# A macaron block on one NeuronCore: silu 1 ahead of the first HH, and attention's batch 0 prepared one round sooner in FFN 1

## The reference, cut to what matters

```python
# x: (8, 1024, 128)
x = x + 0.5 * ffn(layernorm(x))
x = x + attn(layernorm(x))
x = x + 0.5 * ffn(layernorm(x))

def ffn(x):                       # weights: int32 / 127, hidden size 384
    h = silu(x @ wg.T) * (x @ wu.T)
    return h @ wd.T

def attn(x):                      # 4 query heads, 2 key heads of 32
    h = rmsnorm(x) * norm_w
    q, k = l2norm(h @ Wq), l2norm(h @ Wk)
    p = softmax(causal(q @ k.T * exp(log_temperature)))
    return x + gate * ((p @ (h @ Wv)) @ Wo)
```

## Time and profile before

| | us |
|---|---|
| median of 3 runs (459.06 to 459.52) | 459.48 |
| the profiled execution | 459.42 |
| its span, first to last instruction | 457.6 |
| TensorE busy | 413.5 |
| ScalarE busy | 382.8 |
| VectorE busy | 354.2 |
| GpSimd busy | 260.6 |

### The profile page before, as it was taken

How to read it: one execution, slowest core, us unless ns; L and a number is a source line. 1 busy time by engine, 2 the same in 40 slices (tenths; PEclk the granted TensorE clock), 3 DMA queues, 4 the chain that set the end, 5 groups by cost and what they waited for, 6 DMA issues and landing times.

```text
span 457.6 us, 10470 instructions
## 1 busy us (share of the span) xinstructions
PE 413.5 (90%) x3747; PEld 214.1 (47%) x3747; DVE 354.2 (77%) x872; ACT 382.8 (84%) x546; POOL 260.6 (57%) x321
## 2 busy tenths in 40 slices
PE   0779998989998999999999999999999998999995
PEld 0346665663334335335335335345344244767554
DVE  5899997799499789689689689687647937878654
ACT  3799999667968988988988988988977998999961
POOL 5499999973444444444453553541131456998951
PEclk9999999999999999999999999999999999999999
DMA  5586433334026072084072072092070112557462
GB/s 161 127 163 149 65 53 69 70 71 96 20 53 134 1 140 48 1 140 47 0 138 46 0 138 47 1 139 48 1 139 0 24 26 49 136 93 139 93 116 74
DMA packets 119151, 34.94 MB, mean 76 GB/s; under 512 B 101569, under 2 KB 119105, under 8 KB 119105
## 3 DMA queue, kind: packets, MB, share of 16 engines
q1 hardware_dynamic: 117824, 34.02, 38.9%
q10 hardware_dynamic: 1280, 0.33, 0.3%
HBM read 4.98 MB, written 4.19 MB: 20 GB/s over the span
## 4 chain that ended last, share of the span: by engine, by line
PE 51%; issue 14%; ACT 12%; DVE 11%; POOL 7%; DMA 2%; DVEq 0%; SPq 0%; POOLq 0%; ACTq 0%
PE ps L507 11%; PE ps L706 11%; PE ps L687 9%; PE ps L711 9%; ACT XN L458 4%; PE ps L558 3%; PE ps L569 3%; ACT PT L817 3%; PE ps L594 2%; DVE H L327 2%; ACT SG L476 2%; DVE X L1021 2%; PE ps L691 2%; POOL OL L281 2%; DVE AN L1008 1%
## 5 line engine op out<-in xcount | busy, mean ns | idle before, releaser
L817 ACT ACTIVATE PT<-ps,k_exp 128x1024 f32<-128x1024 f32 (+1 forms) x192 | 162.0, 899 | 20.2 <-PE ps L691 14.8
L507 PE MATMUL ps<-XT,WT 128*128 128x512 f16 x384 | 95.0, 386 | 8.6 <-DVE H L327 3.1
L687 PE MATMUL ps<-QKT 128*128 128x512 f16 (+3 forms) x384 | 87.1, 328 | 11.4 <-ACT PT L817 9.3
L706 PE MATMUL ps<-PT,V 128*32 128x512 f32 (+3 forms) x768 | 81.8, 498 | 0.0
L711 PE MATMUL ps<-PT,ones 128*32 128x512 f32 (+3 forms) x768 | 79.6, 486 | 0.0
L433 POOL TENSOR_TENSOR HL<-H,HH 128x1024 f16<-128x1024 f32 x31 | 67.0, 2160 | 7.3 <-ACT HH L482 5.1
L327 DVE SCALAR_TENSOR_TENSOR H<-SG,k_isilu,ps 128x1536 f32<-128x1536 f32 x32 | 58.0, 1811 | 14.9 <-ACT SG L476 5.6
L281 POOL TENSOR_TENSOR OL<-ON,OH 128x512 f16<-128x512 f32 x15 | 18.2, 1216 | 77.4 <-ACT OH L277 77.4
L687 PEld LDWEIGHTS ps<-QKT 128*128 128x128 f16 x384 | 27.8, 97 | 69.2 <-ACT PT L817 60.1
L507 PEld LDWEIGHTS ps<-XT,WT 128*128 128x128 f16 x384 | 34.6, 99 | 54.1 <-issue 14.5
L458 ACT ACTIVATE XN<-X,NB,RS 128x128 f32<-128x128 f32 x128 | 52.4, 482 | 2.7 <-POOL NB L405 2.7
(11 more groups left out here) (139 smaller groups left out, 645.3 us busy)
## 6 DMA issues: line engine op xcount, KB each, us to landing
result<-X SPq DMA_DIRECT2D x15, 256.0 KB, 2.5
...
XT<-w_int SPq DMA_TRANSPOSE x32, 3.1
AXT<-AS SPq DMA_TRANSPOSE x16, 2.8
QKT<-ST SPq DMA_TRANSPOSE x16, 5.6
...
```

The costliest lines, as they stand in the source:

```text
L507: i = e.matmul(out[:, j, :], WT[:, wp, w * NJ + j, :], XT[k % 2][:, xp, :], start=a == 0, stop=a == len(passes) - 1)
L687: i_ = e.matmul(o, QKT[k % 2][:, i // TPC, NH + hp, i % TPC * P:(i % TPC + 1) * P], QKT[k % 2][:, qc, 2 * hp + h, CH - n:CH], start=True, ...
L706: e.matmul(PVD[HD * h:HD * h + HD, 0, CH - n:CH], V[k % 2][:, i, v0:v0 + HD], PT[g % 2][:, h, 0:n], start=i == 0, stop=done, skip_group_ch ...
L817: e.activation(PT[g % 2][:, 2 * hp:2 * hp + 2, 0:n], SCORES[hp][:, :, 0:n], ACT.Exp, scale=k_exp[:, 0:1]).then_inc(a_exp, 1)
```

## The change

- FFN 1 and FFN 2: ScalarE issues silu 1 in the middle of round 0, ahead of HH 0. In FFN 1 VectorE does the moments of block 4 between `low_parts(2)` and `low_parts(3, 4)`. In FFN 2 VectorE itself makes HH 0, and the last reciprocals, product and split move behind rounds 1, 2 and 3; the first up product waits for the copies of the last sums only in its second and third part. TensorE's loop in FFN 1 begins and ends sooner.
- Batch 0 in FFN 1: `normalise` 0 is in round 8 as a whole, the split of x 0 and x 1 is VectorE's (`first_split`, rounds 9 and 11), `turn_x` stands behind `turn_ffn` 12 and 13, the first products behind rounds 10 to 13. V of half 0 comes out by VectorE (rounds 11 and 12), `sums` 0 stand behind round 12, the ten root steps and `unit` 0 in round 13, the ST copies and `sums` of half 1 in round 14. Behind round 15 VectorE does the root steps and `unit` of half 1, the f16 part of ST of half 1 (`first_stack_hi`), its copies, `normalise` 2 and the statistics of block 3.
- The last down product of FFN 1 is cut: its H and HH parts run in FFN 1, its HL part (`down_tail`) behind the first scores; 3 + 3 `keep_running` matmuls stand for 8 + 5.
- Batch 0 of attention: x 2 and x 3 are split by GpSimd alone; the products for batch 1 stand behind groups 4 and 6 (before 3 and 4), `stack_hi` in groups 9 and 10 (before 7 and 8), x 4 and x 5 on ScalarE in group 11 behind the exps of batch 1's group 0 (before in groups 9 and 10); `o_norm` of half 0 stands ahead of the sums, `add_norm` 2 and 3 at the end.

The diff, cut to its changed lines, with some lines of context:

```diff
@@ -170,7 +170,7 @@ semaphores
-        a_xh0, a_fac = sem("a_xh0"), sem("a_fac")
+        a_xh0, a_xh1, a_xl0, a_fac = [sem("a_" + n) for n in ("xh0", "xh1", "xl0", "fac")]
...
@@ -349,7 +349,7 @@ ffn_dve
             def last_h_hi(k, c):
-                if ph and k == NC - 2:
+                if ph and k in (0, NC - 2):
...
@@ -491,18 +491,17 @@ ffn_act
-            early = [(normalise, 0), (normalise, 1), (x_hi, 0), (x_hi, 1), (silu, 0)]
+            early = [(normalise, 0), (normalise, 1), (x_hi, 0), (x_hi, 1), (silu, 0), (silu, 1)]
-            pipeline(e, [(0, silu), (3, normalise), (3, x_hi), (0, amid),
-                         (0, h_hi)],
-                     early)
+            pipeline(e, [(0, silu), (3, normalise), (3, x_hi), (0, amid), (0, h_hi)], early, behind)
-            def products(k, w, out):
+            def products(k, w, out, bank_free=lambda j: None):
+                    bank_free(j)
@@ -527,9 +526,11 @@ ffn_pe
-                if ph and k == 0:
-                    e.wait_ge(a_pvc, 4 * B)
-                products(k, 1, U).then_inc(s_up, 1)
+                def sums_copied(j):
+                    if ph and k == 0 and j:
+                        e.wait_ge(a_pvc, 4 * B - 2 + j)
+                products(k, 1, U, sums_copied).then_inc(s_up, 1)
@@ -537,8 +538,13 @@ ffn_pe
-            def down_of(k, c):
+            def down_tail(k, c):
+                down_of(k, c, (1,))
+            def down_of(k, c, halves=(0, 1)):
+                if not ph and k == NC - 1 and 0 in halves:
+                    halves = (0,)
@@ -554,10 +560,12 @@ ffn_pe
-                for n, (t, j) in enumerate(full):
+                for n, (t, j) in enumerate(full if 0 in halves else []):
+                    if hp not in halves:
+                        continue
...
@@ -581,12 +590,12 @@ ffn_pe
-                ops = dict(gate=gate_, up=up)
+                ops = dict(gate=gate_, up=up, down_tail=down_tail)
-            pipeline(e, [(1, gate_), (-1, down), (0, last_wo), (1, up)], early, after, True, 0 if ph else 2)
+            pipeline(e, [(1, gate_), (-1, down), (0, last_wo), (1, up)], early, after, True, 0 if ph else 4, 8 if ph else 2)
@@ -609,7 +618,7 @@
-        MOVED = {0: [], 1: [], 3: USES[0], 4: USES[1]}
+        MOVED = {0: [], 1: [], 4: USES[0], 6: USES[1], 8: [], 10: USES[8] + USES[10]}
...
@@ -762,6 +771,7 @@ att_pe
+                down_tail()
@@ -772,11 +782,12 @@ att_pe
-                keep_running(8)
+                keep_running(3)
-                keep_running(5)
+                down_tail()
+                keep_running(3)
             def step(k, b):
@@ -792,7 +803,7 @@ att_pe
-                    if k == 0 and g == 3:
+                    if k == 0 and g == 4:
@@ -865,7 +876,6 @@ att_act
-            x_hi(2, 0)
@@ -890,15 +900,16 @@ att_act
-                        if k == 0 and g == 1:
-                            x_hi(3, 1)
-                        g_ = g - 3 if k == 0 else g
+                        g_ = {4: 0, 6: 1}.get(g) if k == 0 else g
-                        g_ = g - 2 if k == 0 else g
+                        g_ = g - 4 if k == 0 else g
-                    if k + 2 < B and g in (9, 10):
+                    if k + 2 < B and k == 0 and g == 11:
+                        x_hi(m0 + 2, 0)
+                        x_hi(m0 + 3, 1)
+                    if k + 2 < B and k >= 1 and g in (9, 10):
@@ -928,13 +939,14 @@ att_pool
             def first_x_hi(m, half):
-                e.tensor_copy(AS[half][:, 0, :, :], AN[half][:, :, :]).then_inc(a_xh0, 1)
+                e.wait_ge(d_x[half], 16)
+                e.tensor_copy(AS[half][:, 0, :, :], AN[half][:, :, :]).then_inc(a_xh1, 1)
             def x_lo(m, half):
-                if isinstance(m, int) and m < 2:
-                    e.wait_ge(a_xh0, m + 1)
+                if isinstance(m, int) and m < 4:
+                    e.wait_ge(a_xh1, m - 1)
-                    e.wait_ge(a_xh, m - 1)
+                    e.wait_ge(a_xh, m - 3)
@@ -947,11 +959,13 @@ att_pool
-                {"rstds_a": rstds_a, "rstds_b": rstds_b, "x_hi": first_x_hi, "x_lo": x_lo,
-                 "stack_lo": stack_lo}[first[0]](first[1], first[1])
+                {"rstds_a": rstds_a, "rstds_b": rstds_b, "stack_lo": stack_lo}[first[0]](first[1], first[1])
+            first_x_hi(2, 0)
+            rstds(3, 3)
+            first_x_hi(3, 1)
             def step(k, b):
@@ -1003,7 +1017,10 @@ att_dve
-                    e.wait_ge(a_xl, m - 1)
+                    if isinstance(m, int) and m < 4:
+                        e.wait_ge(a_xl0, m - 1)
+                    else:
+                        e.wait_ge(a_xl, m - 3)
@@ -1084,6 +1101,26 @@ att_dve
+            def first_split(m):
+                e.wait_ge(a_xn, m + 1)
+                e.tensor_copy(AS[m][:, 0, :, :], AN[m][:, :, :]).then_inc(a_xh0, 1)
+                e.wait_ge(a_xh0, m + 1)
+                e.tensor_tensor(AS[m][:, 1, :, :], AN[m][:, :, :], AS[m][:, 0, :, :],
+                                ALU.subtract).then_inc(a_xl0, 1)
+            def first_v_out(c):
+                src = await_full(e, None, None, ("qkv", 0, c))
+                e.tensor_copy(V[0][:, 2 * c:2 * c + 2, :], src.rearrange("p (t n) -> p t n", t=2))\
+                    .then_inc(a_cp, 1)
+            def first_stack_hi(m):
+                e.wait_ge(a_qn, m + 1)
+                e.tensor_copy(ST[m][:, :, :, 0, :].rearrange("p h t d -> p t h d"), QN[m][:, :, :, :])\
+                    .then_inc(a_hi, 1)
@@ -1118,39 +1155,42 @@ att_dve
             if first == "sums":
-                norms(0, 2, 0, 1, (0, 2))
             if first == "unit":
-                norms(0, 2, 0, 1, (2, 3))
+                norms(0, 2, 0, 1)
             if first == "stack":
+                sums(1, 1)
             if first == "second":
-                sums(1, 1)
+                first_stack_hi(1)
+                stack_hi2(1, 1)
-                stack_hi2(1, 1)
+                stats(3, 3, 3)
             if first == "third":
-                normalise(3, 3, 3)
+                normalise(3, 3, 3)
+                elif what == "split":
+                    first_split(m)
+                elif what == "v_out":
+                    first_v_out(*part)
-            for m in range(2, 4):
-                add_norm(m, m, m)
             def step(k, b):
...
@@ -1174,8 +1216,6 @@ att_dve
                 if nxt:
-                if k == 0:
-                    o_norm(e, b * 2, True)
                 if nxt:
@@ -1190,6 +1230,9 @@ att_dve
                 if nxt:
+                if k == 0:
+                    for m in range(2, 4):
+                        add_norm(m, m, m)
@@ -1223,7 +1266,10 @@ turn_x
         def turn_x(e, m):
-            e.wait_ge(a_xl, m + 1)
+            if m < 2:
+                e.wait_ge(a_xl0, m + 1)
+            else:
+                e.wait_ge(a_xl, m - 1)
@@ -1270,8 +1316,8 @@ sync
-                if c in (13, 14):
-                    turn_x(e, c - 13)
+                if c in (12, 13):
+                    turn_x(e, c - 12)
@@ -1323,10 +1369,7 @@ gpsimd
-                                  9: first(("x_hi", 0), ("x_lo", 0)), 10: first(("x_hi", 1), ("x_lo", 1)),
-                                  11: first(("rstds_a", 2)), 14: first(("stack_lo", 0)),
-                                  15: first(("rstds_b", 3))},
-                     {13: first(("rstds_b", 2), ("rstds_a", 3))})
+                                  12: first(("rstds_a", 2)), 13: first(("stack_lo", 0)), 14: first(("rstds_b", 2))})
@@ -1361,16 +1404,16 @@ scalar
-            ffn_act(e, 0, None, {13: first(("v_out", 0, 0), ("v_out", 0, 1), ("squares", 0)),
-                                 14: first(("v_out", 1, 0)),
-                                 15: first(("stack_hi", 0), ("v_out", 1, 1), ("squares", 1))})
+            ffn_act(e, 0, None, {0: lambda: ffn_act(e, 0, [("silu", 1)]),
+                                 13: first(("v_out", 1, 0)),
+                                 14: first(("stack_hi", 0), ("v_out", 1, 1), ("squares", 1))},
+                    {12: first(("squares", 0))})
-            att_act(e, False, ("stack_hi", 1))
-                ffn_act(e, 1)
+                ffn_act(e, 1, None, {0: lambda: ffn_act(e, 1, [("silu", 1)])})
@@ -1443,12 +1486,16 @@ vector
-            def low_parts():
-                for r in range(2, 5):
+            def low_parts(*parts):
+                for r in parts:
+            def low_parts_and_hidden():
+                low_parts(3, 4)
+                ffn_dve(e, 0, [("hidden", 0)])
@@ -1479,23 +1526,33 @@ vector
+            def split_and_copy():
+                rows("split", 1)()
+                rows("v_out", 0, 0)()
+            def copy_and_stats():
+                rows("v_out", 0, 1)()
+                rows("stats", 2)()
-            ffn_dve(e, 0, None, {-3: low_parts, -2: lambda: ffn_dve(e, 0, [("hidden", 0)]), NC - 1: stage("second")},
```

(36 more changed lines are left out.)

1 line of the change is left out of this document (added).

## The result

The changed kernel takes **467.91 us** (median of 4 runs, 467.34 to 468.28) where the kernel before takes 459.43 in the same comparison (4 runs, 459.06 to 459.52): ratio 1.0189, 95% interval 1.0177 to 1.0202. It is slower by 8.5 us. The forecast was 465.0, range 457 to 469.5. The profiled execution took 467.57 us, 1.9 more than its span of 465.7 (before: 457.6).

The account below looks back on a forecast made before the run. Between hidden 9 and 15 of FFN 1 no engine is free; in attention TensorE is the bound. 459.4 + 4.3 (batch 1's start) + 2.1 (its first product) - 0.8 (FFN 2) = 465.0 us, range 457 to 469.5.

Parts of the forecast that it names:

- First rounds of FFN 1: Start of FFN 1: `hidden` 0 and silu 1 come sooner, -0.4 us (0 to -0.8); hidden 9 at 64.0.
- VectorE in rounds 9 to 14: FFN 1: VectorE's work 27.7 us, meetings (blocking between VectorE and GpSimd) 3.7, waits 1.6; hidden 15 at 97.0.
- The meeting of round 11: FFN 1: VectorE's split 1 blocked by GpSimd; with `weights_low` of round 10, 0 to 3.2 us, taken 0.
- Hidden 15 to exp 4: Into batch 0 of attention: the chain of half 1 takes 16.9 us; exp 4 at 113.9, about where it was.
- Exp 4 to batch 1: Batch 0: products and `stack_hi` two groups later, 29.5 us where it was 25.3; batch 1 starts at 143.4, +4.3.
- the doubt that the prediction named: Ahead of batch 1: if something other than q and k holds TensorE, the forecast is wrong in its mechanism.
- Batch 1: Start of batch 1: its first product comes later, with casts of x 4 and x 5 behind exps: +2.1 us, once.
- FFN 2: Start of FFN 2: up 0 waits less and HH 0 leaves ScalarE: -0.8 us (0 to -1.6).
- The lead that carries through: Rival: no meetings, batch 1 starts 25.4 us behind exp 4, at 133.5; total 455.1, chance 0.22.
- The second rival: No meetings in FFN 1, but 29.5 us from exp 4 to batch 1, at 137.6; total 459.2, chance 0.12.
- The third rival: Every meeting in FFN 1 at full length: hidden 15 at 101.4, batch 1 at 147.8; total 469.4, chance 0.15.

Follow-up runs that it names:

- e5: Changed kernel with GpSimd's HL of rounds 13 to 15 of FFN 1 on 32 of 1024 columns: 463.04 us.
- e9: Changed kernel with GpSimd's HL 13 and 15 held until VectorE's root steps are through, HL 14 until the sums of half 1 are scaled: 465.36 us.
- e1: Changed kernel with batch 1's second product behind group 5 instead of 6 and `stack_hi` behind groups 7 and 8 instead of 9 and 10: 463.39 us.
- e4: Changed kernel with GpSimd making the low part of batch 0's first output ahead of the low parts of q and k: 468.19 us.
- e7: Changed kernel with 14 useless matmuls in TensorE's wait ahead of the first products with wo and 6 behind them: 466.98 us.
- e2: Changed kernel with ScalarE's casts of x 4 and x 5 ahead of the exps of batch 1's group 0: 465.86 us.
- e3: Changed kernel with FFN 2's last split in round 4 and the products with wo in rounds 5 to 7: 465.82 us.
- e12: e11 with `add_norm` of blocks 2 and 3 moved between the sums of half 0 and half 1 of batch 0: 456.40 us.
- e11: Changed kernel with the edits of e1, e2, e3 and e9 together: 459.14 us.

## Why the prediction was right, and where it was not

**First rounds of FFN 1.** Hidden 9 came at 64.04 (64.0), by the path of the forecast: XN 6 waits 0.53 us for GpSimd's factors and starts at 36.04, 0.36 sooner than before.

**VectorE in rounds 9 to 14.** Right in its mechanism and within 0.4 us in its end, 97.36 for 97.0, by terms that were off against each other. The four stretched instructions cost 0.97 (round 9, 1.66 - 0.69), 0.88 (round 11), 1.95 (round 13, 2.13 - 0.18) and 1.54 (round 14, 1.78 - 0.24): 5.3 us, where the sum had 3.7. The meeting of round 11 was taken at 0, that of round 14 at 0.7; `weights_low` of round 10 took 0.55, as before, and met nothing. Work without them was 32.40 - 5.3 = 27.1 (27.7), waits on others 33.32 - 32.40 = 0.9 (1.6). e5 showed the meetings of rounds 13 to 15 to be a cause, and e9, with HL whole, brought hidden 15 to 94.50 as e5 had to 94.30. The Trainium skill's rule (SBUF — State Buffer, Who interferes with whom) says that whichever of the two has the shared ports keeps them for its whole instruction. The root step that ended 0.04 us behind HL agrees, and so does the cast in e9, which ended 0.42 us behind HL and takes 0.56 alone.

**Hidden 15 to exp 4.** 16.68 us (16.9), exp 4 at 114.04 (113.9). Half 1 holds it, as forecast: a root step met HL 15 and took 2.00 us, and TensorE waited 1.68 for the transfer of q and k ahead of exp 4's scores.

**Exp 4 to batch 1.** 29.94 us (29.5): squares of half 1 end 15.0 behind exp 4 (14.6, where the forecast's own terms, 8.8 and two groups of 2.83, make 14.5; the sum goes by the later `stack_hi`), `stack_hi` starts 21.2 behind it (20.9), the scores 8.74 behind that (8.6). e1 gave the distance back by the order alone, e5 left it in place when exp 4 came 4.3 us sooner, and e4 answered the doubt that the prediction named: TensorE waited longest for something other than q and k, but q and k held it.

**Batch 1.** +2.46 (+2.1). With the clock at 1.00 it is 7.40 - 5.54 = 1.86 (e7), of the expected cause (e2: the casts); the other 0.6 us are the clock, which no step had. The step "fewer `keep_running` matmuls cost nothing while TensorE's gaps stay as short as now" asked the right question, at the wrong place: the long gap came ahead of batch 1.

**FFN 2: the step that failed.** Forecast -0.8 (0 to -1.6), measured 7.82 - 7.38 = +0.44. The gains were 0.88 + 0.89 = 1.77, more than taken; what was left out was the split, put behind the norm into one round and so across GpSimd's subtractions (+2.27, e3). The meetings that the prediction priced in FFN 1 were not looked for here, though the earlier trace rows had the 1.60 us of this very subtraction.

**Sum.** Of the 2.9 us by which 467.9 exceeds 465.0, FFN 2 has 1.2, batch 1's start 0.6, its first product 0.4, and the end of the kernel 0.3 (span +8.1 against +7.8 at the last hidden); the rest is the profiled execution against the median.

**The rivals.** The lead that carries through needs a distance of 25.4 from exp 4, and e5 had 29.89 even with most meetings gone. The second rival's picture, no meetings and the chain as computed, is near e5, in which the two splits of rounds 9 and 11 still met: batch 1 at 139.6 against its 137.6, of which 1.0 us had come up to hidden 15 (94.30 for 93.3), 0.6 up to exp 4 and 0.4 behind it. The third rival put hidden 15 at 101.4; it came at 97.36. Its total of 469.4 was nearer the result than 465.0 is, but by the loss in FFN 2, which it did not have.

**Not foreseen at all**: the two moved `add_norm`. In the changed kernel's trace ScalarE's second squares of batch 1 wait for nothing (157.73) and TensorE waits 0.66 us, as in e12, since batch 1 was late for other reasons. Once these were mended they cost 2.7 us (e11 to e12), the fallen clock behind the wait included.
